# The gated layer with ternary weights: seven block products in place of eight

## The reference

```python
# layer 1: x = layernorm(x + f(x)); f is a Mamba-2 block with a residual, then
#   h + silu(h2 @ gate_w.T) * (h2 @ up_w.T) @ down_w.T      (all dense fp32, inner size 1792)
# layer 2, which the change is about (x is [2, 512, 512], I = 1376):
def _bitlinear(x, w):
    scale = mean(abs(w))
    q = round(clip(w / (scale + EPS), -1, 1))      # -1, 0 or 1
    return x @ (q * scale).T
gate, up = _bitlinear(x, w_gate), _bitlinear(x, w_up)
out = _bitlinear(gate * up, w_down)
x = layernorm(x + out)
```

## Time and profile before

| | |
|---|---|
| median of three runs | 491.06 us |
| the profiled execution, its span | 491.12 us, 489.4 us |
| mean granted TensorE clock | 0.997 |
| down projection of layer 1, batch 1 | 319.90 to 359.65 |
| gate and up, batch 0 (with four turns) | 359.65 to 402.34 |
| its down projection | 402.34 to 422.34 |
| gate and up, batch 1 | 422.34 to 463.40 |
| its down projection | 463.40 to 483.36 |
| after the last matmul | 483.36 to 489.40 |

### The profile page before, as it was taken

One profiled execution on the slowest core, in us unless ns is written; L12 is line 12 of the kernel. 1 busy time (PEld: TensorE's weight loads), 2 busy tenths in 40 slices (PEclk: granted clock), 3 DMA queues, 4 the chain that ended last, 5 costly groups with the idle time before them and its releaser, 6 DMA issues.

```text
span 489.4 us, 6246 instructions
## 1 busy us (share of the span) xinstructions
PE 473.6 (97%) x2112; PEld 379.1 (77%) x2112; DVE 312.8 (64%) x530; ACT 236.3 (48%) x446; POOL 207.4 (42%) x240
## 2 busy tenths in 40 slices
PE   7979999998999899999999999999999999999995
PEld 7867677876767777888788888888888888888884
DVE  3797577635588667676898899866959523411233
ACT  4687857777657567454443254224815530032300
POOL 5494356533573587867877100010005342133321
PEclk9999999999999999999999999999999999999998
DMA  7622022011222415343322346511210000100001
GB/s 239 236 86 85 3 86 66 9 36 64 87 87 86 151 64 177 148 143 115 131 71 103 129 135 214 170 43 38 99 58 1 0 1 13 73 2 1 1 18 68
DMA packets 14431, 40.80 MB, mean 83 GB/s; under 512 B 2368, under 2 KB 2368, under 8 KB 14400
## 3 DMA queue, kind: packets, MB, share of 16 engines
q1 hardware_dynamic: 14400, 40.41, 24.6%
HBM read 38.30 MB, written 2.10 MB: 83 GB/s over the span
## 4 chain that ended last, share of the span: by engine, by line
PE 84%; DVE 8%; POOL 3%; ACT 2%; issue 2%; DMA 1%; POOLq 0%; DVEq 0%; ACTq 0%
PE psA L1668 8%; PE psA L1669 8%; PE psA L1452 6%; PE psA L1454 5%; PE psB L1678 4%; PE psB L1677 4%; PE psA L1440 3%; PE psA L1458 3%; PE psA L1460 3%; PE psA L1445 3%; PE psA L1441 3%; PE psA L1647 3%; PE psA L1643 3%; PE psB L1647 3%; PE psB L1643 3%; PE psA L1646 3%
## 5 line engine op out<-in xcount | busy, mean ns | idle before, releaser
L1668 PE MATMUL psA<-xT_h,q_gu 128*128 128x512 f32 x176 | 70.1, 398 | 0.0
L1669 PE MATMUL psA<-xT_l,q_gu 128*128 128x512 f32 x176 | 69.1, 393 | 0.0
L683 POOL TENSOR_SCALAR var<-mv 128x1 f32<-128x1 f32 x16 | 4.9, 304 | 127.7 <-DVE mv L1089 127.6
L1060 ACT ACTIVATE gate_t<-psA 128x512 f32<-128x512 f32 x22 | 13.1, 598 | 75.1 <-PE psA L1669 75.1
L835 POOL TENSOR_TENSOR int_l<-prod_t,int_h 128x512 fp32r<-128x512 f32 x22 | 28.9, 1314 | 43.6 <-ACT int_h L1065 43.6
L1404 DVE TENSOR_TENSOR prod_t<-gate_t,psA 128x512 f32<-128x512 f32 x22 | 15.1, 689 | 48.9 <-PE psA L1669 46.3
L745 POOL TENSOR_TENSOR beta<-wsum,beta 128x512 fp32r<-128x512 f32 x28 | 35.9, 1302 | 24.1 <-ACT beta L911 24.1
L1668 PEld LDWEIGHTS psA<-xT_h,q_gu 128*128 128x128 f32 x176 | 33.1, 188 | 8.1
L1669 PEld LDWEIGHTS psA<-xT_l,q_gu 128*128 128x128 f32 x176 | 33.1, 188 | 7.4
L1440 PE MATMUL psA<-xT_h,win_h 128*128 128x512 f32 x80 | 32.7, 408 | 3.0 <-DVE xbc L1207 3.0
L1677 PE MATMUL psB<-q_dn,int_h 128*128 128x512 f32 x88 | 34.3, 389 | 0.0
(11 more groups left out here) (255 smaller groups left out, 1355.4 us busy)
## 6 DMA issues: line engine op xcount, KB each, us to landing
raw<-in_f_gu_t SPq DMA_DIRECT2D x22, 512.0 KB, 3.5
raw<-in_w_gu_t SPq DMA_DIRECT2D x14, 512.0 KB, 3.6
raw<-in_f_dn_t SPq DMA_DIRECT2D x10, 512.0 KB, 3.5
raw<-in_w_gu_t SPq DMA_DIRECT2D x14, 256.0 KB, 2.9
raw<-in_w_dn_t SPq DMA_DIRECT2D x7, 512.0 KB, 3.4
raw<-in_w_in_t SPq DMA_DIRECT2D x5, 512.0 KB, 4.1
x<-in_hidden SPq DMA_DIRECT2D x8, 256.0 KB, 5.2
out<-x SPq DMA_DIRECT2D x8, 256.0 KB, 2.0
```

Source lines behind the costliest of these rows:

```text
L1668: nc.tensor.matmul(ps, w, seq(xT_h, k, b), start=k == 0, stop=False)
L1669: done = nc.tensor.matmul(ps, w, seq(xT_l, k, b), start=False, stop=k == KD - 1)
```

## The change

Gate and up of both batches become one product of 2x2 blocks. The block rows are gate and up (a11, a12 and a21, a22 by halves of the depth, 256 each), the block columns the batches (b11, b21 and b12, b22). Seven products per tile f replace eight, each with 256 of depth, 128 features and 512 rows, four matmuls. ACT widens only what is used plain (w1: a11 and a12, five slots; w22: a22, three slots), POOL makes four ternary sums straight from q8. t12, t34 are the differences of the turned input, made from the banks of ("turn3", c) and from xT_full, an unsplit copy of batch 0's turned rows that ACT now makes too.

Products are not put together on DVE alone: ACT copies product fa(f) out, goes on to copy the sum fa + fb, and later writes the copy of fa into another bank (step "fopen"). On that bank PE adds f6, f7 and f4 one after the other, ACT copying it out in between (u3 after f6, v3 after f7). f5 and f3 stand in a bank of psB.

The last four tiles of down, batch 1, are taken chunk by chunk ("downlast") so that batch 1's chunks end one after the other. ffndown of batch 0 runs tile by tile over four banks, that of batch 1 chunk by chunk. The ternary weights of down get a tile of their own, q8_dn.

The steps (`-` lines of the loops that go away are left out):

```diff
+    steps += [("act", 1, FM - 2), ("act", 1, FM - 1),
+              ("downlast", 0), ("ln1a", 4), ("ln1", 4),
+              ("downlast", 1), ("ln1a", 5), ("ln1", 5), ("ln1x", 4),
+              ("downlast", 2), ("ln1a", 6), ("ln1", 6), ("ln1x", 5), ("turn3", 0), ("thigh3", 0),
+              ("downlast", 3), ("ln1a", 7), ("ln1", 7), ("t3", 0), ("t4", 0), ("ln1x", 6), ("tlow3", 0), ("turn3", 1),
+              ("fa", 0), ("fa", 1), ("thigh3", 1), ("ln1x", 7), ("tlow3", 1), ("t3", 1), ("t4", 1), ("turn3", 2),
+              ("fb", 0), ("thigh3", 2), ("fa", 2), ("fb", 1), ("tlow3", 2), ("t3", 2), ("t4", 2), ("turn3", 3),
+              ("thigh3", 3), ("fa", 3), ("fb", 2), ("t3", 3), ("tlow3", 3), ("fa", 4), ("fb", 3),
+              ("t3high", 0), ("t3high", 1), ("t3high", 2), ("t3high", 3), ("fb", 4), ("fopen", 0), ("t4", 3),
+              ("t3low", 0), ("t3low", 1), ("t3low", 2), ("t3low", 3), ("b22low", 0), ("b22low", 1), ("b22low", 2)]
+    for f in range(FF):
+        steps += [("f6", f), ("f5", f)]
+        if f == 0:
+            steps += [("t4high", c) for c in range(NC)] + [("t4low", c) for c in range(NC)] + [("b22low", 3)]
+        else:
+            steps.append(("f4", f - 1))
+        if f + ALF < FF:
+            steps += [("wide1", f + ALF), ("fa", f + ALF)]
+        if f == FF - 1:
+            steps.append(("widedn", 0))
+        steps.append(("f7", f))
+        if f >= 1:
+            steps.append(("f3", f - 1))
+        if f + ALF < FF:
+            steps.append(("fb", f + ALF))
+        if f + 1 < FF:
+            steps.append(("fopen", f + 1))
+        if f >= 1:
+            if f + SUM_SLOTS - 1 < FF:
+                steps += [("wide22", f + SUM_SLOTS - 1), ("fsum", f + SUM_SLOTS - 1)]
+            steps.append(("split", 0, f - 1))
...
+    steps += [("widedn", 1), ("f4", FF - 1), ("f3", FF - 1), ("split", 0, FF - 1)]
```

ACT, on its side:

```diff
+                    if kind == "ln1t":
+                        s.wait_ge(*done_p("p3", FM - 1))
+                        nc.scalar.activation(plain_x(t), bank_b(step).rearrange("p (k q) -> p k q", k=KD), ACT.Copy)
...
+                elif kind == "fa":
+                    f = at[0]
+                    s.wait_ge(*done_p("fa", f))
+                    nc.scalar.activation(p1_0[:, f, :], bank_a(("fal", f)), ACT.Copy).then_inc(fe_ready, 1)
+                elif kind == "fb":
+                    f = at[0]
+                    s.wait_ge(*done_p("fb", f))
+                    nc.scalar.activation(int0[:, f, :], bank_a(("fal", f)), ACT.Copy)\
+                        .then_inc(freed_a(("fal", f))[0], 1)
+                elif kind == "fopen":
+                    f = at[0]
+                    job = ("fx", f)
+                    s.wait_ge(fe_ready, f + 1)
+                    s.wait_ge(a_free[JOB_A[job] % 4], JOB_A[job] // 4)
+                    nc.scalar.activation(bank_a(job), p1_0[:, f, :], ACT.Copy).then_inc(fx_open, 1)
```

PE (fb, f5, f3, f4 have the same form, with waits for fe_ready, nothing, s4w_ready and fc22_ready, w22_ready and fv_ready):

```diff
+            def exact_product(ps, weights, moving, opens):
+                high, low = moving
+                for k in range(2):
+                    nc.tensor.matmul(ps, weights[:, chunk(k)], high[:, k, :], start=opens and k == 0, stop=False,
+                                     skip_group_check=not opens)
+                    done = nc.tensor.matmul(ps, weights[:, chunk(k)], low[:, k, :], start=False, stop=k == 1,
+                                            skip_group_check=not opens)
+                done.then_inc(p_done, 1)
...
+                elif kind == "fa":
+                    pe.wait_ge(w1_ready, f + 1)
+                    exact_product(open_a(("fal", f)), w1[:, f % ALF, 0:2 * P], moving_x(0, 0), True)
+                elif kind == "f6":
+                    pe.wait_ge(s12w_ready, f + 1)
+                    pe.wait_ge(fx_open, f + 1)
+                    exact_product(bank_a(("fx", f)), ternary_sum(f, 2), moving_ft(1), False)
+                elif kind == "f7":
+                    pe.wait_ge(s3w_ready, f + 1)
+                    pe.wait_ge(fu_ready, f + 1)
+                    exact_product(bank_a(("fx", f)), ternary_sum(f, 0), moving_x(1, 0), False)
```

More of the change, by code:

```diff
@@ L46 @@
 NPRE = 11
+ALF = 5
+SUM_SLOTS = 3
+LAST = 4
 def build_schedule():
@@ L218, in build_schedule @@
                ("ln1t", 0), ("ln1a", 3), ("ln1", 3), ("ln1x", 2), ("ln1t", 1), ("ln1x", 3), ("ln1t", 2), ("ln1t", 3)]
-    for f in range(FM):
-        if f + 2 < FM:
-            steps.append(("act", 1, f + 2))
+    early = [("wide1", f) for f in range(ALF)] + [("wide22", f) for f in range(SUM_SLOTS)]
+    for f in range(FM - LAST):
+        steps.append(("act", 1, f + 2))
         steps.append(("down", 1, f))
@@ new lines, in build_schedule @@
+    assert ALF == 5 and not early
+    for f in range(FF):
[19 more added lines that the diff above has]
+            steps.append(("split", 0, f - 1))
+            if tern and not halves:
@@ L248, in build_schedule @@
                 loads_now, halves = ternary()
                 steps += loads_now
-            if b == 0 and halves:
+            if halves:
                 steps.append(halves.pop(0))
[L252 to L258, removed]
+    steps += [("widedn", 1), ("f4", FF - 1), ("f3", FF - 1), ("split", 0, FF - 1)]
@@ new lines, in build_schedule @@
+    wide = [("widedn", p) for p in range(2, FF // 2 + 1)]
+    split = [("split", 1, f) for f in range(FF)]
+    for f in range(FF):
+        steps.append(("ffndown0", f))
+        steps += wide[:1] + split[:2]
+        wide, split = wide[1:], split[2:]
+    for c in range(NC):
+        steps += [("ffnsum", 0, c), ("ln2", 0, c)]
+    for c in range(NC):
+        steps += [("ffndown1", c), ("ffnsum", 1, c)]
+        if c >= 1:
+            steps.append(("ln2", 1, c - 1))
+    steps.append(("ln2", 1, NC - 1))
@@ L259, in build_schedule @@
+    assert not (wide or split)
+    assert not (sums or tern or between or parts or halves)
     return steps, loads
@@ L301, in psum_jobs @@
             b += ([("st", *at)] if at[1] < NC - 1 else []) + [("y", *at)]
-        elif kind in ("outproj", "turn2", "ffndown"):
+        elif kind in ("outproj", "turn2"):
             b.append((kind, *at))
+        elif kind == "ffndown0" and at[0] == 0:
+            b.extend(("ffndown", 0, c) for c in range(NC))
+        elif kind == "ffndown1":
+            b.append(("ffndown", 1, *at))
         elif kind == "down" and at[1] == 0:
@@ L527, in turned_b1, with turned_x, plain_x, int_plain @@
             return bank_b(("turn2", 1, c)).rearrange("p (k q) -> p k q", k=KD)
+        def turned_x(c):
+            return bank_b(("turn3", c)).rearrange("p (k q) -> p k q", k=KD)
+        def plain_x(c):
+            return xT_full[:, :, L + c * P:L + (c + 1) * P]
+        def int_plain(b, f):
+            if b:
+                return plain1_first[:, f, :] if f < 7 else plain1_last[:, f - 7, :]
+            return int0[:, f, :]
+        def int_parts(b, f):
+            if b:
+                return int1_h[:, f, :], (int1_first[:, f, :] if f < 7 else int1_last[:, f - 7, :])
+            return int0_h[:, f, :], int0_l[:, f, :]
+        def tern_made(what, f):
+            return tern_ready, [LOADS[n] for n in TERN].index((what, f)) + 1
+        def halves_seen(f):
+            return actl_ready, FM + f + 1
         def heads(tile):
@@ L1047, in _ @@
                     p = at[0]
-                    s.wait_ge(*completed(("down", NB - 1, NC - 1)))
-                    s.wait_ge(tern_ready, [LOADS[n] for n in TERN].index(("qdn", p)) + 1)
+                    s.wait_ge(*tern_made("qdn", p))
+                    s.wait_ge(*(done_p("f5", FF - 1) if p < 2 else done_p("f4", FF - 1)))
                     nc.scalar.activation(q_dn[:, 2 * p:2 * p + down_width(p) // D, :],
[L1051 to L1065, removed]
@@ L1067, in _ @@
+                                         by_tile(q8_dn[:, p, 0:down_width(p)]), ACT.Copy).then_inc(qdn_ready, 1)
         @block.vector
@@ L1414, in _ @@
-                    v.wait_ge(*freed_b(step))
+                        .then_inc(freed_b(job)[0], 1)
+                    v.wait_ge(*freed_b(job))
                     statistics(t, NT + t)
@@ L1648, in _ @@
                         if f == FM - 1:
-                            last.then_inc(a_done if b else b_done, 1)
+                            last.then_inc(b_done, 1)
                         elif c == NC - 1:
                             last.then_inc(act_free, 1)
+                elif kind == "downlast":
+                    c = at[0]
+                    ps = bank_a(("down", 1, c))
+                    for f in range(FM - LAST, FM):
+                        n = FM + f
+                        if c == 0:
+                            pe.wait_ge(actl_ready, n + 1)
+                        high, low = dn_tile(f)
+                        act_high, act_low = act_hl[:, n % ACT_SLOTS, 0, chunk(c)], act_hl[:, n % ACT_SLOTS, 1, chunk(c)]
+                        nc.tensor.matmul(ps, act_high, high, start=False, stop=False)
```

(12 more changed lines are left out.)

307 lines of the change are left out of this document (262 added, 45 removed).

## The result

The changed kernel takes 506.5 us (median of four runs, 506.17 to 508.64) against 491.02; the ratio is 1.032, 95% interval 1.029 to 1.035. The profiled run took 506.22 us with a span of 504.5. The forecast was 499.8, its range ended at 506. The direction and the main term were right; 6.7 us were missing.

The account below looks back on a forecast made before the run. PE, busy 97% of the span, was taken to bound the kernel. Stalls of 19.8 us less 11.1 saved gave +8.7 on the profiled run's 491.12 us, so 499.8 us; range 493 to 506.

Parts of the forecast that it names:

- main term: f6(1) to f6(6) wait for ACT's bank opening, queued behind the copy of fb: 6 x 1.47 = 8.8 us.
- removed matmuls: Gate and up: 308 matmuls instead of 352 on a full PE, 11.1 us saved.
- unit: One wait at f6 behind ACT's copy of fb and the opening: 1.47 us including PE's restart, the bank write taken as 0.63.
- four late openings: For f = 6 to 9 the opening follows the copy of f7(f), partly covered by f3(f-1): 4 x 0.54 = 2.2 us.
- entry of ffndown0: Its fourth bank is freed late by DVE after f3(10): a stall of 0.8 us (0 to 1.5).
- transition: Between down of batch 1 and iteration 0: one stall of 3.2 us (2 to 5), all placed at f6(0).
- rival A: Openings are hidden if fopen(f+1) ends before the last matmul of fb(f+5): 488.8 us, faster; 11%.
- rival C: PE's clock falls in the new gaps; 40 matmuls at 1.2 GHz cost another 9 us: 509 us; 7%.
- downlast(0): Deferred tiles of down, batch 1: PE waits for the last activation tiles, DVE slowed by POOL's sums: 3.0 us (0 to 5.5).
- fa(5): In iteration 0, fa(5) waits for ACT to widen its weights, f5(0) covering part: 1.8 us (1 to 2.5).
- first opening: f6(0) waits for ACT's opening, queued behind work on chunk 3's differences, there at about 8.1 us: 3.2 us (2 to 5).
- high ends: All stalls at their upper bounds, 27.3 us, less 10.3 saved: +17 us.

Follow-up runs that it names:

- openings-early kernel: Changed kernel with the opening of bank fx(f+1) moved ahead of ACT's copies of fb(f+5) and f7(f); 493.07 us.
- filled waits: Changed kernel with spare PE transposes of the identity in front of five waits: three in downlast(0), one each ahead of f6(0) and fa(5); 502.63 us.
- kernel with late sums: Changed kernel with POOL's first three sets of ternary sums moved out of the down projection, to later places; 500.87 us.
- no opening: Changed kernel without ACT's copy of fa into bank fx and its part of the sums; f6 opens its bank itself; 492.54 us.
- first opening early: Changed kernel with fopen 0 right behind the copy of fa(4) and wide1(5) behind that of fb(3); 500.49 us.
- splits first: Changed kernel with the last two activation splits moved ahead of the last quantisation in the down projection; 503.45 us.

## Why the prediction was wrong

**What held.** PE was full, so the removed matmuls counted in full (-10.7 against -11.1: the mean pitch was 0.2319, not 0.2306). The queue's order (the opening behind fb's copy) and its unit were right within 3%: 1.51 against 1.47, with ACT's write to a bank at 0.60, inside the bound 0.5 to 0.7. The four late openings, the entry of ffndown0 and the transition came within 0.6 us each. The openings-early kernel shows that rival A's point, fopen ahead of fb's end, is where it decides.

**The step that failed** is the clock. The sum had it at nothing, on one row of before: a wait of 3.0 us with a granted clock of 1.00; rival C had 7%. In the changed kernel it fell behind the waits in downlast(0) and again behind the one at f6(0), and cost 4.0 us, more than half of the 6.7 that were missing. The same 3.0 us wait early in the kernel was itself followed by a fall in the changed kernel's run:

```profile
35.00:40.00 5.00, 4.09 (x12) 3.27 (x13) 4.88 (x7) 3.36 (x5) 2.19 (x3) 0.70 0.00 0
```

The row of before was one outcome of two, read as a rule. The Trainium skill (TensorE: Matmul & The Clock Gate, "HAM oscillation — how this bites in real kernels") says that idle stretches between bursts return the array to the lower clock; the filled waits agree (granted clock 1.00, 3.5 us less). Rival C's price, 9 us for 40 matmuls, was too high: 20 ran at the lower clock.

**Mis-sized terms.** downlast(0), 3.0 against 4.0: the prediction let POOL's sums hold up only the quantisations, and took 1.8 us for it; the splits L1548 have two SBUF inputs as well. Four of them at 1.13 instead of 0.69 make 1.8 us and five quantisation steps 1.6, 3.4 us in all between 340.97 and 352.69, and the kernel with late sums lost 2.9 us of the wait. The Trainium skill's sentence on two SBUF inputs (SBUF — State Buffer, "Who interferes with whom") covered these too, and this trace agrees (1.13 against 0.69). It does not cover L1559, which reads one tile and slowed too (0.87 against 0.48); why is not shown. fa(5), 1.8 against 1.0: f5 ran at the lower clock and hid more; with early openings, where it ran at full clock, the wait was 1.8 with its restart. In the transition the waits at fb(2) and fb(3), 1.5 us, were seen in part only; they are ACT copies of fa behind thigh3. The prediction had the whole 3.2 at f6(0), where 2.3 were measured.

**Slips in the working.** The bounds 0.5 to 0.7 of a copy give 8.0 to 9.2 for the six openings, not 7.2 to 9.6. DVE's items ahead of chunk 3's differences add up to 7.8, not 8.1, which would make the first opening 2.9. The high ends add up to 27.1, not 27.3. None of these moves the forecast by more than 0.3 us.

**The range** ended at 506, 0.5 us short: the lower clock stood in a rival and not among the unknown costs of the forecast. The prediction's own high ends, +17, reach 508; the range was drawn narrower.

## What to carry to other kernels

In an engine's written order, look at what stands between a result that is long ready and the one who waits for it: here ten openings cost 11.4 us of waits; six of them stood 3.3 us behind ACT's copy of fa, where 0.5 was possible. Their place and that of a few other steps decided between 8 us gained and 15 lost. Where a change adds waits of one or two us to a TensorE that was full, charge some us for the clock behind them, and don't take one trace without a fall for a promise. When POOL gets work beside a full DVE, charge every DVE instruction with two SBUF inputs, not only those seen slow before.

## What the runs showed of the hardware

A fall of TensorE's clock is not settled by the wait alone. The early wait of 2.8 to 3.1 us, in code that is the same in all kernels, was followed by a granted clock of 1.00 (35 to 40 us) in seven profiled runs, the kernel before's among them, and of 0.60 to 0.70 in three: the changed kernel, sums late, no opening. In these three the stretch begins at 320.2 to 322.2 us, in the other seven at 318.6 to 319.8, so such a fall is part of what varies ahead of it. The kernel before has runs of that kind too: four of its 30 runs beside the groups took 493.6 to 494.0 us, with a mean clock of 0.991 against 0.993 to 0.997 in the rest.

Of the waits in downlast(0) (0.6, 2.1 and 1.0 us), the clock fell behind all three in the changed kernel and with no opening, and behind the first two, before the third began or with no third, in openings early, first opening early and splits first (granted clock 0.87, 0.90 and 0.94 from 351 to 352, 0.50 from 352 to 353). It did not fall when one of 0.8 was left (sums late). Behind the 2.2 us at f6(0) it fell in the changed kernel, sums late and splits first, and did not in openings early, where 1.7 us at fa(5) followed. No wait of PE for another engine was over 3.1 us. What decides between the two outcomes stays open.

ACT writes 128x512 into a bank in 0.60 us, as long as it takes to read one (0.60); within SBUF it takes 0.62. PE's products on such a bank keep their pitch (62.28 us for 266 matmuls, 62.32 without the written banks).
